# Attention with routed experts on one core: selector matmuls replaced by DMA copies, a spread load and a product on GpSimd

## What is computed

```python
qh = layernorm(x).reshape(b, 8, 16, lq);  kh = vh = ctx.reshape(b, 8, 16, lk)
s = SCALE * log(k_length)[:, None, None, None]
attn = softmax(s * einsum('bhdq,bhdk->bhqk', qh, kh), axis=-1)
x = x + einsum('bhqk,bhdk->bhdq', attn, vh).reshape(b, hd, lq)
# then, with n = layernorm(x): the 2 best of 8 experts per token,
#   silu(n w1') * (n w3') w2', weighted, added to x
```

## Time and profile before

| | |
|---|---|
| median of three runs | 1286.69 us (1286.11 to 1287.01) |
| span of the profiled execution, first to last instruction | 1285.3 us; the page gives no other time of this execution |
| TensorE (PE) busy | 1125.7 us, 88% |
| VectorE (DVE) | 590.4 us, 46% |
| ScalarE (ACT) | 449.9 us, 35% |
| GpSimd (POOL) | 606.7 us, 47% |
| attention part, to the first load of an expert's tile | 580 us |
| mean granted TensorE clock | 0.957 of full speed |

### The profile page before, as it was taken

The page is one execution under the profiler, slowest core; times in us unless marked ns, Lnnn a source line. Parts: engine busy times, 40 slices in busy tenths (PEclk is TensorE's granted clock), DMA queues, the critical chain, the costliest instruction groups (busy, mean ns, idle before and its releaser), DMA issues.

```text
span 1285.3 us, 20411 instructions
## 1 busy us (share of the span) xinstructions
PE 1125.7 (88%) x5561; PEld 472.8 (37%) x5562; DVE 590.4 (46%) x884; ACT 449.9 (35%) x812; POOL 606.7 (47%) x547
## 2 busy tenths in 40 slices
PE   1899999999999999727999999999999999999810
PEld 0223333333333332213555554455455555544300
DVE  5877787877788875131222222222222222222245
ACT  3266666666666666611111111111111111111200
POOL 6434666666666541126504707428281473800045
PEclk9999999999999999958999999999999999999965
DMA  6454555555555441024203305124241333310157
GB/s 181 148 167 141 168 168 168 164 162 158 159 159 165 138 133 45 19 98 159 99 33 131 123 25 196 65 98 163 98 163 33 131 130 123 122 33 33 34 158 259
DMA packets 87243, 158.92 MB, mean 124 GB/s; under 512 B 13696, under 2 KB 52608, under 8 KB 81792
## 3 DMA queue, kind: packets, MB, share of 16 engines
q1 hardware_dynamic: 73728, 90.23, 22.9%
q0 software_dynamic: 12896, 67.12, 14.9%
q10 hardware_dynamic: 576, 1.05, 0.2%
HBM read 107.50 MB, written 50.86 MB: 123 GB/s over the span
## 4 chain that ended last, share of the span: by engine, by line
PE 75%; DVE 8%; DMA 6%; issue 5%; ACT 4%; POOL 2%; SPq 1%; DVEq 0%; POOLq 0%; ACTq 0%; PEldq 0%
PE rows L1048 30%; PE heads_out L1048 15%; PE heads_out L951 7%; PE scores L938 6%; PE rows L924 6%; ACT W L559 3%; DVE nm L682 3%; DMA W<-parts_dram 3%; PE scores L1081 2%; PE misc L1000 2%; DMA U<-expert_out_dram,fidx 1%; PE misc L1021 1%; PE misc L1040 1%; PE misc L977 1%; POOL U L523 1%
## 5 line engine op out<-in xcount | busy, mean ns | idle before, releaser
L1048 PE MATMUL rows<-W,U 128*128 x1776 | 392.1, 381 | 4.6 <-issue 3.0
L559 ACT ACTIVATE W<-scores 128x512 f32<-128x512 f32 x512 | 282.9, 598 | 160.2 <-PE scores L938 155.0
L682 DVE TENSOR_REDUCE nm<-rows 128x2 f32<-128x1024 f32 x256 | 305.5, 1220 | 58.3 <-PE rows L924 41.3
L1048 PEld LDWEIGHTS rows<-W,U 128*128 128x128 bf16 x1776 | 174.5, 98 | 208.9 <-issue 9.7
L1048 PE MATMUL heads_out<-W,U 128*128 x888 | 200.3, 383 | 5.2 <-issue 5.1
L924 PE MATMUL rows<-W,U 96*128 96x512 bf16 x512 | 163.7, 404 | 44.8 <-DMA W<-parts_dram 25.8
L865 DVE TENSOR_TENSOR U<-rows,U 128x512 f32<-128x512 f32 x78 | 53.8, 691 | 318.9 <-ACT U L627 318.9
L938 PE MATMUL scores<-U,W 128*128 128x512 bf16 x512 | 180.3, 387 | 13.9 <-ACT W L559 4.8
L400 POOL TENSOR_TENSOR W<-U,W 128x2048 bf16<-128x2048 f32 x42 | 171.0, 4072 | 7.7 <-POOL W L399 7.7
L627 ACT ACTIVATE U<-rows 128x512 f32<-128x512 f32 x78 | 46.4, 598 | 331.0 <-PE rows L1048 329.9
L951 PE MATMUL heads_out<-W,U 128*32 128x512 f32 x1024 | 138.0, 611 | 0.1
(11 more groups left out here) (144 smaller groups left out, 780.5 us busy)
## 6 DMA issues: line engine op xcount, KB each, us to landing
U<-wpack_dram POOLq DMA_DIRECT2D x42, 1024.0 KB, 5.2
parts_dram<-U SPq DMA_DIRECT2D x32, 384.0 KB, 4.1
U<-parts_dram SPq DMA_DIRECT2D x32, 384.0 KB, 3.9
W<-parts_dram SPq DMA_DIRECT2D x32, 384.0 KB, 5.1
U<-slots_dram SPq DMA_DIRECT2D x39, 256.0 KB, 2.6
expert_out_dram<-U SPq DMA_DIRECT2D x39, 256.0 KB, 2.1
parts_dram<-U SPq DMA_DIRECT2D x32, 256.0 KB, 3.9
stage<-wpack_dram POOLq DMA_DIRECT2D x12, 512.0 KB, 5.3
```

Source lines behind the costliest of these rows:

```text
L559: s.activation(probs[:, w % 2, j, kk, :], sc[u % 2][:, :], ACT.Exp) \
L682: v.tensor_reduce(nm[:, bb.parity, 2 * k:2 * k + 2], p1[k % 2][:, :].rearrange("p (c k) -> p c k", c=2), AX_X, ALU.max, negate=True).then_ ...
L1048: ins = m.matmul(bank, stat[:, s_part, k, :], W[:, bass.ds(at_w, 512)], start=(k == 0 and n == 0), stop=(k == n_chunks - 1 and n == 2))
```

## The change

The two selector products, ScalarE's copy and VectorE's product go. SyncE copies the eight head blocks from `og` to `us` with eight DMAs from SBUF to SBUF, issued between the store of the sums and the load of the denominators. The load of the reciprocals, until now 8 rows, repeats each row 16 times into a 128-row tile `rb`. GpSimd multiplies `us` by `rb` in place, and adds x. ScalarE waits for `us_in` before it overwrites `og`. The selectors' setup on GpSimd goes. Beside it the table of tile bounds gets a copy `tile_at` with -1 in its first place, so that each expert counts at least one tile.

```diff
@@ sync
                     for g in range(2):
                         sp.dma_start(sums_dram[bass.ds(pv.n, 1), 4 * g:4 * g + 4].rearrange("o h q -> (o h) q"),
                                      og[16:113:32, g, :]).then_inc(S["sums_out"], 16)
+                    if b.within(2, B):
+                        sp.wait_ge(S["x1_ready"], b.n - 1)
+                    for h in range(H):
+                        sp.dma_start(us[h * DH:(h + 1) * DH, :], og[32 * (h % 4):32 * (h % 4) + DH, h // 4, :]) \
+                            .then_inc(S["us_in"], 16)
                     sp.wait_ge(S["sums_out"], b.n * 32)
...
-                    if b.within(2, B):
-                        sp.wait_ge(S["r_ready"], b.n - 1)
-                    sp.dma_start(r8[:, :], recips_dram[bass.ds(pv.n, 1)].rearrange("o h q -> (o h) q")) \
-                        .then_inc(S["rec_in"], 16)
+                    sp.dma_start(rb[:, :], recips_dram[bass.ds(pv.n, 1)].rearrange("o h q -> (o h) q")
+                                 .unsqueeze(1).to_broadcast([H, DH, L])).then_inc(S["rec_in"], 16)
@@ gpsimd
+                    hold(S["us_in"], b.n * 128)
+                    hold(S["rec_in"], b.n * 16)
+                    g.tensor_tensor(us[:, :], us[:, :], rb[:, :], ALU.mult).then_inc(S["t_ready"], 1)
                     hold(S["t_ready"], b.n)
...
-                    g.tensor_tensor(x1[:, :], xr, tb[:, :], ALU.add).then_inc(S["x1_ready"], 1)
+                    g.tensor_tensor(x1[:, :], xr, us[:, :], ALU.add).then_inc(S["x1_ready"], 1)
@@ scalar
                     if bb.within(1, B - 1):
-                        act.wait_ge(S["u_ready"], bb.n)
+                        act.wait_ge(S["us_in"], bb.n * 128)
                         act.wait_ge(S["sums_out"], bb.n * 32)
...
-                exps(1, range(0, 4))
-                if pv.within(0, B - 1):
-                    act.wait_ge(S["u_ready"], b.n)
-                    if pv.within(1, B - 1):
-                        act.wait_ge(S["t_ready"], b.n - 1)
-                    s.activation(us[:, :], misc[:, :], ACT.Copy).then_inc(S["us_ready"], 1)
-                exps(1, range(4, 8))
+                exps(1, range(0, 8))
@@ vector
-                st = Steps(dve.wait_ge, S["table_chain"], 0, 5)
+                st = Steps(dve.wait_ge, S["table_chain"], 0, 7)
...
+                st.step(v.tensor_copy(tile_at[:, :], tio[:, 1, 0:B]))
+                st.step(v.memset(tile_at[:, 0:1], -1.0))
...
-                if pv.within(0, B - 1):
-                    dve.wait_ge(S["r_ready"], b.n)
-                    dve.wait_ge(S["us_ready"], b.n)
-                    if pv.within(1, B - 1):
-                        dve.wait_ge(S["x1_ready"], b.n - 1)
-                    v.tensor_tensor(tb[:, :], misc[:, :], us[:, :], ALU.mult).then_inc(S["t_ready"], 1)
@@ tensor
-                        if (w, u) == (1, 2) and behind:
-                            if reader:
-                                pe.wait_ge(*reader)
-                            pe.wait_ge(S["og_ready"], b.n * 2)
-                            for gr in range(2):
-                                ins = m.matmul(misc[:, :], selu[:, gr, :], og[:, gr, :], start=(gr == 0),
-                                               stop=(gr == 1))
-                            ins.then_inc(S["u_ready"], 1)
-                            reader = (S["us_ready"], b.n)
...
-                        if (w, u) == (3, 1) and behind:
-                            pe.wait_ge(S["rec_in"], b.n * 16)
-                            if reader:
-                                pe.wait_ge(*reader)
-                            m.matmul(misc[:, :], selb[:, :], r8[:, :], start=True, stop=True).then_inc(S["r_ready"], 1)
-                            reader = (S["t_ready"], b.n)
```

More of the change, by code:

```diff
@@ L122, in build @@
         us = sb("us", [P, L], F32)
-        tb = sb("tb", [P, L], F32)
+        rb = sb("rb", [P, L], F32)
         x1 = sb("x1", [P, L], F32)
@@ L126, in build @@
         zt = sb("zt", [P, KD, P], F32)
-        selu = sb("selu", [P, 2, P], F32)
-        selb = sb("selb", [8, P], F32)
-        r8 = sb("r8", [8, L], F32)
         den = sb("den", [P, 32], F32)
@@ L157, in build @@
         tio = sb("tio", [P, 2, T + 1], F32)
+        tile_at = sb("tile_at", [P, B], F32)
         upto = sb("upto", [P, E, E], F32)
@@ L193, in build @@
             prep_steps keys_steps first_keys z_steps route_a_steps route_b_steps queries_out keys_out
-            sums_out rec_out m_out den_in rec_in m_in cv_in p1_ready p1_used scores_ready exp_done pv_done
-            og_ready vt_ps vt_ready u_ready us_ready r_ready t_ready x1_ready x1_kept zt_ps zt_ready
+            sums_out rec_out m_out den_in us_in rec_in m_in cv_in p1_ready p1_used scores_ready exp_done pv_done
+            og_ready vt_ps vt_ready t_ready x1_ready x1_kept zt_ps zt_ready
             gate_ready gate_used mask_ready rank_ready rank_used idx_ready rec_ready st1_steps
@@ L219, in slots @@
                 body(Batch(b // 2, b % 2, b, b))
-        N_CONST = 10
+        N_CONST = 7
         block = cx.enter_context(nc.Block())
@@ L371, in constants @@
                 g.memset(ident[:, :], 0.0).then_inc(k, 1)
-                g.memset(selu[:, :, :], 0.0).then_inc(k, 1)
-                g.memset(selb[:, :], 0.0).then_inc(k, 1)
                 g.memset(ltri[:, :], 1.0).then_inc(k, 1)
                 g.memset(vt, 0.0).then_inc(k, 1)
-                hold(k, 5)
+                hold(k, 3)
                 g.affine_select(out=ident[:, :], in_=ident[:, :], compare_op=ALU.not_equal, fill=1.0, base=0,
                                 pattern=[[-1, P]], channel_multiplier=1).then_inc(c, 1)
-                for gr in range(2):
-                    v = selu[:, gr, :].rearrange("p (h d) -> p h d", h=H)
-                    g.affine_select(out=v, in_=v, compare_op=ALU.not_equal, fill=1.0, base=128 * gr,
-                                    pattern=[[-32, H], [-1, DH]], channel_multiplier=1).then_inc(c, 1)
-                v = selb[:, :].rearrange("p (h d) -> p h d", h=H)
-                g.affine_select(out=v, in_=v, compare_op=ALU.not_equal, fill=1.0, base=0,
-                                pattern=[[-1, H], [0, DH]], channel_multiplier=1).then_inc(c, 1)
                 g.affine_select(out=ltri[:, :], in_=ltri[:, :], compare_op=ALU.is_gt, fill=0.0, base=0,
@@ L795, in _ @@
             slots(dve, slot)
-            st = Steps(dve.wait_ge, S["table_chain"], 1, 5)
+            st = Steps(dve.wait_ge, S["table_chain"], 1, 7)
             link = st.step
@@ L813, in _ @@
             link(v.tensor_tensor(k3, cnt.unsqueeze(2).to_broadcast([P, E, B]),
-                                 tio[:, 1, 0:B].unsqueeze(1).to_broadcast([P, E, B]), ALU.is_gt))
+                                 tile_at[:, :].unsqueeze(1).to_broadcast([P, E, B]), ALU.is_gt))
             link(v.tensor_reduce(tiles, k3, AX_X, ALU.add))
@@ L954, in values @@
                         ins.then_inc(S["pv_done"], 1)
-                reader = (S["t_ready"], b.n - 1) if pv2.within(0, B - 1) else \
-                    (S["m_ready"], b.n + 1) if full else None
+                reader = (S["m_ready"], b.n + 1) if full else \
+                    (S["rank_used"], b.n - 2) if b.within(B, B + 1) else None
                 for w in range(4):
```

## The result

| | before | after |
|---|---|---|
| median | 1286.85 us (1286.11 to 1288.69) | 1332.49 us (1327.91 to 1334.11) |
| profiled execution | 1285.3 us span | 1332.53 us, span 1330.9 us |
| x1 of slot 1 starts at | 105.26 us | 108.87 us |
| x1 of slot 12 | 447.37 us | 492.57 us |
| last x1 | 556.82 us | 602.65 us |

The change makes the kernel slower by 3.5% (ratio 1.0348, 95% interval 1.0334 to 1.0362). Forecast were 1283 us and faster. All of the loss lies in the attention part, which ends 45.9 us later; the profiled spans differ by 45.6. By x1: slot 1 is 3.6 us later, the eleven steady slots after it add 41.6 (383.70 against 342.11, 34.9 each against 31.1), and what follows adds 0.6.

The account below looks back on a forecast made before the run. TensorE was read as busy 88% of the span, but GpSimd's loop as limiting steady slots. Terms 1.6 - 1.5 - 2.6 - 3.0 - 1.5 + 2.5 + 0.4 = -4.1 gave span 1281.2, median 1283 us; range 1273 to 1294.

Parts of the forecast that it names:

- start and slot 1: Start: two small steps in VectorE's table chain, +0.4 us; selector setup 0; slot 1, with reload late, 0.
- steady slots 2 to 12: Attention part's steady slots: each 0.15 to 0.2 us longer, summed as 11 x 0.15 = +1.6 us.
- slots 13 to 16: Last attention slots, where TensorE's saving was to arrive: -1.5, -2.6, -3.0 and -1.5 us.
- tail, last sums to x1's end: Attention's end, nothing hidden: denominators +2.2, spread load +1.7, product and gaps -1.4, together +2.5 us.
- What is added on SyncE: Eight copy issues, 3.4 us together, hidden in a steady slot; query parts' store to 308.2, reload to 311.8, spread load at 318.7.
- The spread load: Reciprocals' load of 256 KB before GpSimd's product: 3.3 us in quiet, 3.7 beside the scatter; ends 2.7 and 3.8.
- The step behind it: GpSimd's loop from slot to slot, ending in z before TensorE's transposes, has only some 0.5 us to spare.
- Size of the issue: Each SyncE copy issue taken as 0.42 us, from 0.30 to 0.67; eight take 3.4 us, ends 2.4 and 5.4.
- rival (a): Spread load lands late for GpSimd, at 4.5 us adding 0.8 a steady slot: 1293 us, chance 0.2.
- Rival (d): SyncE's issues at 0.67 us: VectorE stands 0.8 us at the reciprocal each steady slot, 1292 us, chance 0.08.
- The signs by which I said I would be wrong: GpSimd waiting over 0.5 us for the spread load, denominators late, or steady slots under 30.5 us.

Follow-up runs that it names:

- run 4: Changed kernel with its eight copies issued later by SyncE: four behind the query parts' stores, four behind the reciprocals' store; 1293.76 us, ratio 1.0043.
- run 3: Kernel before with eight copies added in the change's place, into a tile that is then overwritten, nothing removed; 1320.5 us, ratio 1.0266.
- run 8: Changed kernel with four copies left in the change's place and four moved behind the reciprocals' store; 1306.47 us, ratio 1.0155.
- run 2: Kernel before with only the spread load of the reciprocals and GpSimd's product; first selector product and ScalarE's copy kept; 1305.22 us, ratio 1.0138.
- run 10: Changed kernel with four copies behind the query parts' stores, then the reciprocals' store, ahead of the reload, and four copies behind the reload; 1282.98 us, ratio 0.9969.
- run 7: Changed kernel with the load of the denominators issued ahead of the eight copies; 1343.11 us, ratio 1.0433.
- run 15: Changed kernel with the gather through DRAM (one store, one load) in late places and the reciprocals' store ahead of the reload; 1286.29 us, ratio 0.9994.
- run 6: Changed kernel with GpSimd's load of a 512 KB weight chunk issued behind its scatter, not ahead of its products; 1341.6 us, ratio 1.0428.
- run 9: Changed kernel with the reciprocals' store issued ahead of the wait for the parts and of the reload; 1313.79 us, ratio 1.0207.

## Why the prediction was wrong

The forecast's sum was -4.1 us; the trace has +45.9, which splits so:

| term | forecast | measured |
|---|---|---|
| start and slot 1 | +0.4 | +3.6 |
| steady slots 2 to 12 | +1.6 | +41.6 |
| slots 13 to 16 | -8.6 | -4.4 |
| tail, last sums to x1's end | +2.5 | +5.0 |

The tail is measured from the last of ScalarE's copies to the end of the last x1: 545.73 to 558.09 before, 586.51 to 603.92 after. Slots 13 to 16 are what is left of the 0.6. Of the 3.6 at the start run 4 gives back 2.9, so they are the copies' place too; `tile_at` was in no run by itself.

**The step that failed** is the one under "What is added on SyncE" that the parts' store "waits for GpSimd until 307.1 anyway and moves to about 308.2", the reload comes at 311.8, and the spread load "is issued at about 318.7, as the load of r8 is now". I followed the copies through one slot in absolute times and let the waits of before absorb them: 1.2 us while the sums are under way, 1.6 until GpSimd has the query parts (305.52 to 307.12), the rest until TensorE has made its scores. Measured from the sums' store, us:

| | before | forecast | after, first slot | second slot |
|---|---|---|---|---|
| stores of the query parts | 4.5 | 5.6 | 7.4 | 7.4 |
| reload | 9.4 | 9.2 | 11.0 | 13.7 |
| store of the reciprocals | 10.4 | not given | 12.0 | 14.7 |
| load of the reciprocals | 16.3 | 16.1 | 17.6 | 19.6 |
| x1 | 20.6 | 21.3 | 22.9 | 25.1 |

The reload, put at -0.2 us, moved by +1.6 and +4.3, and with it what stands behind it. Of the 2.3 and 4.6 us by which x1 comes later, 1.3 and 3.3 are there when the load of the reciprocals is issued; the other 1.0 and 1.3 are the spread load and the product. In the second slot 2.5 us of it are the landing of the stores beside GpSimd's load of the weight chunk (4.4 us of waiting against 1.9). Runs 3, 4 and 8 show the price: place and number of the copies alone make 12.7 to 38.7 us.

**The step behind it** is the reading that GpSimd's loop "has only some 0.5 us to spare" and is what limits. I looked for the loop that turns slowest and found GpSimd's own list. The loop that runs through three engines and SyncE (sums, denominators, reciprocals' store of 5.9 us, load, product, x1, ScalarE's copy, exponentials) I had in pieces, each with its cover, and never added round. Run 2 shows that it had hardly any slack: 1.8 us more from the sums to x1 cost 1.9 us a slot.

**A term that isn't there** is the clock. The sum takes TensorE at full speed throughout; in the steady slots of the changed kernel it was granted 0.94, and of the 38.5 us between it and run 10 in these slots 12 to 15 are that.

**Size of the issue.** A copy is 0.59 us, 0.625 with the gap to the next; I took 0.42 within 0.30 to 0.67. Together 5.0 against 3.4, inside the ends that I gave. These 1.6 us are most of the 1.8 by which the stores of the query parts missed the forecast. But at 3.4 us the kernel would have lost too: run 8 has 2.5 us of early issues and loses 12.7 against run 4, and an estimate on the line from there to the changed kernel gives 22 us for 3.4. Rival (d), "SyncE's issues at 0.67", had VectorE standing 0.8 us for the denominators. It stands 0.97 and 1.50 in the two slots above, and run 7, which cures that, is slower. The Trainium skill (Perfetto Trace Analysis, What "DMA-bound" means) keeps a busy issuing sequencer apart from busy DMA engines and says that such a window is the making of descriptors; the trace agrees: SyncE full for 5.00 us, from 299.05 and again from 333.86, at a DMA share of 0.17 in both stretches, each copy landing 2.0 us after its issue.

**The spread load.** In steady slots 3.49 and 3.72 us, 3.7 forecast: right. In the quiet of slot 15 and the tail 4.17 and 3.88, 3.3 forecast, upper end 3.8: too low. With the eight engines of the rule from the Trainium skill (DMA: Bandwidth & Descriptors, Why a DMA increments its semaphore by 16 and not by 1) in rival (a) the estimate there would be 3.8; the measured times are nearer to that than to 2.68. No run changed the number of engines. The tail's +5.0 is 3.9 for the issues (forecast 2.2), 2.3 for the load (1.7), 0.2 for the denominators' landing and -1.4 for product and gaps (-1.4).

**Rivals.** (a) had the place right, GpSimd waiting for the spread load (28.3 us in eleven steady waits), and put it down to the load's length; it was more its start (1.3 and 3.3 us) than load and product (1.0 and 1.3). (a) and (d) together, at their own prices, give 1302. The signs by which I said I would be wrong were the right ones: GpSimd waits over 0.5 us, denominators late.

**What was right.** In the first slot shown TensorE stands about 2 us ahead of a late score (1.83) and ScalarE about 2 us for x1 (2.26); over the eleven steady slots ScalarE's waits for x1 are 15.4 us in nine. The product takes 1.27. VectorE's short idle time behind the reciprocal is gone. None of it decided anything. Slots 13 to 16 did get shorter, by half of what was forecast.

## What to carry to other kernels

Before pricing an insertion in a queue, list what is queued behind it and follow each item to the end of its loop, across engines and into the next iteration; add the loop up, DMA landings included, and compare it with the slot. Issue time on SyncE is work on one engine like any other: eight small copies were 5 us of it, and where they stood in the list was worth 39 us, more than the first selector product that they replaced (1.72 us a batch, 28 us in all). An issue that is moved forward gains nothing if its transfer is under way so much the longer beside large ones, as the spread load of run 15. And price a wait that comes round in every slot with the clock that follows it: here 0.5 to 0.8 us more for each us. Fewer and larger DMAs, behind those that somebody waits for, made a slower idea into a slightly faster kernel (0.9952 for the gather alone through DRAM, 0.9969 for the full change with late copies and the reciprocals' store first).

## What was not expected of the hardware

A copy of 16 rows of 2 KB from SBUF to SBUF takes SyncE 0.59 us to issue; the loads in SyncE's list of the kernel before take 0.25 to 0.42, the load that repeats 8 rows 0.72, and one store of 512 KB 0.45. The bytes don't set it. A load of 16 KB took 0.37 us to issue, and 0.51 when it stood right behind the eight copies. The reciprocals' store, 16 KB, is 4.0 to 7.3 us under way behind the reload's 768 KB (runs 6 and 4), 2.0 ahead of it (run 9's median) and 1.4 in the tail. The spread load, 256 KB, takes 3.5 to 4.0 us when the parts are in, and 8.7 to 9.6 right behind reload and gather (run 15). A TensorE wait of 1.83 us was followed by 3.4 us at half clock, one of 2.27 us by none.
